# Moving the first two batches' output projection, x1, norm and turn of h2 from the layer stage into the second scan's side work

## The reference, cut to what matters

```
def step(state, xs):                       # the scan, for every batch
    d_t, B_t, C_t, u_t = xs
    dA = jnp.exp(d_t[..., None] * A)
    state = state * dA + (d_t * u_t)[..., None] * B_t[:, None, :]
    y_t = jnp.einsum('ben,bn->be', state, C_t)
...
attn_out = jnp.einsum('hst,thd->shd', att, v).reshape(S, N_HEADS * HEAD_DIM) @ wo
x1 = x + attn_out
h2 = _rms_norm(x1, ln2_w)
mlp = jax.nn.silu(h2 @ w_gate) * (h2 @ w_up) @ w_down
processed = x1 + mlp
gated = gate * processed + (1.0 - gate) * x
```

## Time and profile before

| | us |
|---|---|
| median of 3 runs | 2834.7 (2831.01 to 2835.09) |
| the profiled execution's own time | 2834.77 |
| its span in the profile | 2833.0 |
| PE busy | 2541.2 (90%) |
| PEld busy | 1845.5 (65%) |
| DVE busy | 1963.8 (69%) |
| ACT busy | 1614.7 (57%) |
| POOL busy | 1614.6 (57%) |

### The profile page before, as it was taken

One profiled execution on the slowest core, in us unless ns is written; L12 is line 12 of the kernel. 1 busy time (PEld: TensorE's weight loads), 2 busy tenths in 40 slices (PEclk: granted clock), 3 DMA queues, 4 the chain that ended last, 5 costly groups with the idle time before them and its releaser, 6 DMA issues. The chain is left out here.

```text
span 2833.0 us, 38276 instructions
## 1 busy us (share of the span) xinstructions
PE 2541.2 (90%) x13528; PEld 1845.5 (65%) x13528; DVE 1963.8 (69%) x2505; ACT 1614.7 (57%) x3478; POOL 1614.6 (57%) x898
## 2 busy tenths in 40 slices
...
GB/s 274 254 90 83 74 146 70 123 113 68 141 76 68 153 382 266 285 151 129 105 103 159 105 105 169 93 105 186 93 53 283 286 152 49 89 156 151 154 152 101
DMA packets 249629, 410.43 MB, mean 145 GB/s; under 512 B 50656, under 2 KB 134624, under 8 KB 246624
## 3 DMA queue, kind: packets, MB, share of 16 engines
...
...
## 5 line engine op out<-in xcount | busy, mean ns | idle before, releaser
L696 POOL TENSOR_TENSOR s_x<-s_hp,k_bC 128x1024 f32<-128x1024 f32 x288 | 680.1, 2367 | 48.9 <-DVE s_hp L1152 48.8
L677 POOL TENSOR_TENSOR s_x<-s_du,k_bB 128x1024 f32<-128x1024 f32 x254 | 600.6, 2376 | 13.9 <-DVE s_du L1178 7.6
L803 PE MATMUL s_py<-k_ident,s_x 128*128 128x128 f32 x4096 | 525.1, 274 | 31.1 <-POOL s_x L696 31.0
L803 PEld LDWEIGHTS s_py<-k_ident,s_x 128*128 128x128 f32 x4096 | 462.7, 142 | 46.5 <-POOL s_x L696 42.7
L1076 ACT ACTIVATE s_pA<-s_delta,k_negA 128x512 f32<-128x512 f32 x512 | 333.6, 681 | 172.4 <-DVE s_x L1129 166.9
L1822 PE MATMUL l_p<-l_hT,l_ring 128*128 128x256 f32 x1792 | 389.7, 381 | 1.9 <-ACT l_hT L1928 1.0
L1822 PEld LDWEIGHTS l_p<-l_hT,l_ring 128*128 128x128 f32 x1792 | 342.2, 191 | 49.2 <-issue 1.4
L1076 ACT ACTIVATE s_x<-s_delta,k_negA 128x512 f32<-128x512 f32 x512 | 340.2, 710 | 0.0
L1152 DVE TENSOR_TENSOR_SCAN s_hp<-s_x,s_carry,s_pA 128x512 f32<-128x512 f32 x256 | 321.6, 1267 | 21.8 <-PE s_pA L785 16.1
L977 ACT ACTIVATE s_xT<-s_duT,k_BT 128x128 f32<-128x128 f32 x1024 | 336.4, 389 | 0.1
L1152 DVE TENSOR_TENSOR_SCAN s_hp<-s_x,s_pA 128x512 f32<-128x512 f32 x256 | 309.9, 1211 | 33.8 <-ACT s_x L1076 22.1
...
(10 more groups left out here) (218 smaller groups left out, 3718.9 us busy)
## 6 DMA issues: line engine op xcount, KB each, us to landing
k_bC<-scratch_xd SPq DMA_DIRECT2D x32, 1024.0 KB, 10.4
scratch_ug<-p_ug ACTq DMA_DIRECT2D x16, 1024.0 KB, 4.2
...
```

The source lines that it names most:

```text
L677: pool.tensor_tensor(out=x[:, 4 * g:4 * g + 2], in0=du[:, s % 2:s % 2 + 1].broadcast_to([P, 2, HALF]), in1=bB[:, 2 * g:2 * g + 2], op=ALU. ...
L696: pool.tensor_tensor(out=x[:, 2 * i:2 * i + 2], in0=hp_of(s, i), in1=bC[:, 2 * i:2 * i + 2], op=ALU.mult).then_inc(pool_hc, 1)
L803: last = nc.tensor.matmul(py[:, a], x[:, n, a * P:(a + 1) * P], ident[:], is_transpose=True, start=False, stop=n == NS - 1 and a == HALF / ...
```

## The change: what it does, and the diff

Layer 1 ends with the attention. Its output o stays in `hidden[:, 16:32]`. SP stores the raw base rows and the normed rows `hid` to scratch and loads what scan 2 starts with as soon as the queue gets there, before k, coef and v.

Scan 2 gets 26 slots in a unit instead of 21, in an order of its own: the output projection of the left 512 columns of the result (64 slots, 32 matmuls of 512 columns, from slot 0 in unit 0 to unit 2), a gap of 7 slots, that of the right 512 columns (64 slots, to unit 5), a gap of 40 slots, in which x1, base, mean square, power, norm, and the turn of h2 (16 transposes, units 5 and 6) take place, then gate and up (512 slots, from unit 6 to 26), a gap of 10, and down (128 slots, to unit 31). Before, gate and up ran from unit 0 to 24 and down to unit 30. `wo` comes through the same ring, 16 tiles of 512 KB in the place of 16 tiles of the same size in layer 1. h2T's memory holds the base rows until they are stored. The diagonals of B lie in the tensor of `bB` now; both scans make and use them as before, and the helpers that take `first` give the same numbers for both.

```diff
-FILL = (1, 5, 3, 3, 1, 2, 2, 4)
+FILL = (1, 5, 4, 3, 3, 3, 3, 4)
...
+TILES_WO = H2 * NH // 2
+TILES_UP = TILES_WO + 2 * NI
+TILES_ALL = TILES_UP + NI // 2
+WO_PART = 2 * NH * SPAN
+WO_DONE_0 = fill_slot(WO_PART - 1)
+WO_FROM = (0, fill_from(WO_DONE_0 + 3))
+WO_DONE = (WO_DONE_0, fill_slot(WO_FROM[1] + WO_PART - 1))
+X1_LAG, BASE_LAG = 1, 2
+SQUARE_AT, MEAN_AT, POW_AT, NORM_AT = (WO_DONE[1] + k for k in (4, 4, 5, 8))
+TURN_AT, SPREAD_AT = (WO_DONE[1] + 8, WO_DONE[1] + 10), (WO_DONE[1] + 10, WO_DONE[1] + 12)
 GATE_UP = 2 * NI * KT
-TILES_UP, TILES_ALL = 2 * NI, 2 * NI + NI // 2
+GATE_UP_FROM = fill_from(WO_DONE[1] + 13)
 DOWN_HALF = 2 * NI * SPAN
-DOWN_FROM = GATE_UP + 10
+DOWN_FROM = GATE_UP_FROM + GATE_UP + 10
...
             if fill:
-                sp.dma_start(h2T[:].rearrange("p k r -> p (k r)"), t["h2T0"]).then_inc(h2_in, 16)
-                sp.dma_start(coef[:], t["coef0"]).then_inc(coef_in, 16)
                 for k in range(RING):
                     load_weights(k)
+                sp.dma_start(hid, t["hid0"].rearrange("(a p) c -> p a c", p=P)).then_inc(hid_in, 16)
+                sp.dma_start(base, t["base0"].rearrange("(a p) c -> p a c", p=P)).then_inc(base_in, 16)
...
+                if fill and s == (WO_DONE[1] + BASE_LAG) // NPAIR:
+                    sp.wait_ge(base_ready, H2 * SPAN)
+                    sp.dma_start(t["base0"].rearrange("(a p) c -> p a c", p=P), base).then_inc(base_out, 16)
...
+            def wo(h, k):
+                head, a = k // SPAN, k % SPAN
+                tile = h * NH // 2 + head // 2
+                if k == 0 and h:
+                    pe.wait_ge(x1_ready, SPAN * h)
+                    pe.wait_ge(base_ready, SPAN * h)
+                if k % (2 * SPAN) == 0:
+                    pe.wait_ge(w_in[tile % RING], 16 * (tile // RING) + 16)
+                last = nc.tensor.matmul((p_gate, p_up)[a][:], o[:, head, a * P:(a + 1) * P],
+                                        ring[:, tile % RING, head % 2 * HALF:(head % 2 + 1) * HALF], start=head == 0, stop=head == NH - 1)
+                if k % (2 * SPAN) == 2 * SPAN - 1:
+                    last.then_inc(w_used, 1)
+
+            def turn_h2(j):
+                if j == 0:
+                    pe.wait_ge(x1_ready, SPAN * H2)
+                    pe.wait_ge(base_ready, SPAN * H2)
+                    pe.wait_ge(normed, SPAN)
...
+            def square(b):
+                act.wait_ge(x1_ready, SPAN + b + 1)
+                nc.scalar.activation(normed_rows[:, b], hid[:, b], ACT.Square, accum_out=squares[:, b:b + 1]).then_inc(sq_ready, 1)
...
+            def spread(j, i):
+                act.wait_ge(h2_turned, j + 1)
+                act.wait_ge(ln2_in, 16)
+                act.wait_ge(base_out, 16)
...
     T_DOWN = T_MLP + 2 * NI
-    TILES = T_DOWN + NI if last_half else T_MLP
+    TILES = T_DOWN + NI if last_half else T_WO
...
-                sp.wait_ge(base_ready, 3 * SPAN)
+                sp.wait_ge(base_ready, SPAN)
                 sp.dma_start(t["base0"].rearrange("(a p) c -> p a c", p=P), rows[:]).then_inc(out_done, 16)
-                sp.wait_ge(h2_act, KT // 2)
-                sp.wait_ge(h2_vec, KT // 2)
-                sp.dma_start(t["h2T0"].rearrange("p (k r) -> p k r", r=ROWS), hT[:]).then_inc(out_done, 16)
+                sp.wait_ge(hid_ready, SPAN)
+                sp.dma_start(t["hid0"].rearrange("(a p) c -> p a c", p=P), hid[:]).then_inc(out_done, 16)
...
-            pe.wait_ge(expd, COMBOS)
-            for k in range(NH - APART):
...
-            turn(normed_rows, h2row_ready, turned2)
-
-            if last_half:
+            if last_half:
+                pe.wait_ge(expd, COMBOS)
+                for k in range(NH - APART):
```

More of the change, by code:

```diff
@@ L75, in __init__, with states_by_pool, quad_place @@
         self.ropes = ctx.enter_context(nc.sbuf_tensor(f"c{first}_ropes", [P, SPAN, 2 * DH], F32))
+TURNED, SCALED = (3, 7), {0: (1, 5), SPAN: (1, 5)}
+def states_by_pool(first):
+    return [n for n in range(NS) if n // 2 not in TURNED + SCALED[first]]
+def quad_place(first, g):
+    mine = states_by_pool(first)
+    quad = [n for n in mine if n // 4 == g]
+    return mine.index(quad[0]), len(quad)
 class Kept:
@@ L85, in sb @@
             return ctx.enter_context(nc.sbuf_tensor("k_" + name, shape, F32))
-        self.bB = sb("bB", [P, NS // 2, HALF])
+        self.bB = sb("bB", [P, max(len(states_by_pool(first)) + 2 * len(SCALED[first]) for first in SCALED), HALF])
         self.bC = sb("bC", [P, NS, HALF])
@@ L346 @@
 NPAIR = NS // 2
-FROM_PE = (1, 3, 5, 7)
-TURNED, SCALED = (3, 7), (1, 5)
-FROM_POOL = tuple(i for i in range(NPAIR) if i not in FROM_PE)
-NT, NF, ND_B = 2 * len(TURNED), 2 * len(FROM_PE), 2 * len(SCALED)
+NT = 2 * len(TURNED)
 HP_BUFS = 3
@@ L412, in scan_stage @@
     carry = sb("carry", [P, NE, NS])
+    if scaled:
+        free = len(states_by_pool(first))
+        diagB = bB[:, free:free + ND_B].rearrange("p n (a q) -> p n a q", q=P)
     pA = bank("pA", [P, 4, HALF])
@@ L431, in scan_stage @@
         hidden = keep.hidden
+        o = hidden[:, NH:2 * NH]
+        hid, normed_rows = (hidden[:, KT * k:KT * (k + 1)].rearrange("p m r -> p (m r)").rearrange("p (b d) -> p b d", d=DI) for k in range(2))
+        base = h2T[:].rearrange("p k r -> p (k r)").rearrange("p (b d) -> p b d", d=DI)
+        ln2 = sb("ln2", [P, KT])
+        squares = sb("squares", [P, SPAN])
+        minus_half = sb("minus_half", [P, SPAN])
         ring = sb("ring", [P, RING, KT * P])
@@ L473, in after_vec @@
     def after_vec(s, i):
[L474 removed]
+        return vec_count[s, i]
     def after_carry(s, i):
@@ L690, in times_C @@
             def times_C(s, i):
-                if i not in pool_pairs(s):
+                if i not in pool_pairs(first, s):
                     return
@@ L728, in _ @@
                     begin(s + 1)
-                if last_tile:
-                    make_diagonals(chunk(s) + 1, 1)
+                if last_tile and scaled:
+                    make_diagonals(chunk(s) + 1, scaled[0])
+                if fill:
+                    root(NPAIR * s, NPAIR * s + NPAIR // 2)
                 times_C(s, 3)
@@ L735, in _ @@
                 times_C(s, 5)
-                if last_tile:
-                    make_diagonals(chunk(s) + 1, 5)
+                if last_tile and scaled:
+                    make_diagonals(chunk(s) + 1, scaled[1])
                 quad(s + 1, 1)
@@ L784, in make_b @@
                         else:
-                            last = nc.tensor.matmul(out, duT[:, a * P:(a + 1) * P], diagB[:, 2 * SCALED.index(i) + n % 2, a], start=True, stop=True)
+                            last = nc.tensor.matmul(out, duT[:, a * P:(a + 1) * P], diagB[:, 2 * scaled.index(i) + n % 2, a], start=True, stop=True)
                     last.then_inc(b_ready, 1)
@@ L838, in feed_forward @@
                 for k in range(begin, end):
-                    if k < GATE_UP:
-                        gate_up(k)
+                    for h in range(H2):
+                        if 0 <= k - WO_FROM[h] < WO_PART and (k - WO_FROM[h]) % 2 == 0:
+                            wo(h, (k - WO_FROM[h]) // 2)
+                    if 0 <= k - GATE_UP_FROM < GATE_UP:
+                        gate_up(k - GATE_UP_FROM)
                     at = k - DOWN_FROM
```

297 lines of the change are left out of this document (192 added, 105 removed).

## The result

| | before | changed |
|---|---|---|
| median, us | 2832.86 (2829.88 to 2835.09, 4 runs) | 2810.97 (2808.05 to 2813.41, 4 runs) |
| ratio to before | | 0.9925, interval 0.9910 to 0.9941 |
| the profiled execution's own time | 2834.77 | 2810.57 |
| its span | 2833.0 | 2808.7 |
| first scan of scan 2, to the first scan of unit 31 | 791.2 | 833.4 |

The change makes the kernel 22 us faster by the medians and 24.2 by the two profiled executions. Three sections of the trace account for the difference of the spans: scan 2's first scan starts 67.7 us earlier (1248.02 instead of 1315.74), the 32 units take 42.3 us more (859.44 instead of 817.17, unit 31 taken as 26.0 in both), and what follows them takes 1.1 more (701.2 instead of 700.1).

What follows compares the result with a forecast made beforehand. It took PE to become the bound of nearly every scan 2 unit; -64 us from layer 1 and +46 in scan 2 made -18 on 2834.77, with 1 us for side-chain gaps 2818 us; 8 in 10 range 2798 to 2834.

Steps and rivals of the forecast that it cites:

- What goes from layer 1: End of layer 1: scan 2 starts at 1243.0, 65.3 us earlier; less 1 us for stores, net -64 (-60 to -65).
- a late end of layer 1: Rival: a store, the kept loads or wv's tiles land after the attention; by 10 us it gives 2828; chance 0.05.
- PE becomes the bound: Scan 2's 23 units with 26 slots: PE needs 26.3 us, taken as 26.6 with waits, 612 us in all.
- The light units: Scan 2's units 2, 5, 6 and 26: PE has room, DVE or ACT bounds; 103 us, ends 98 and 108.
- The late tile: Chunk starts: tile issued behind eight column loads, so PE waits 1 to 3 us in unit 8, up to 5 in 16.
- The four first units: Units 0, 8, 16 and 24, which start chunks: 27.2, 30.5, 35 and 29.3, together 122 us, ends 117 and 132.
- The sum: Whole kernel: scan 2's units 863 us against 817.17, +46; with -64 from layer 1, -18 on 2834.77.
- The range: The forecast's own ends: -65 + 37 to -60 + 62, thus 2807 to 2836, mostly 2808 to 2829.
- The signs named ahead: Scan 2 starts near 1243; units 9-15, 17-23 at 26.3 to 27 us; DVE's L1118 wait far above 19.4; unit 5 at most 26.5.
- PE has room: Rival: scan 2 stays bound by DVE and POOL and grows by some 15 us, giving 2786; chance 0.14.
- the rule weighed in the prediction: Skill's rule, not followed: read weight-load share, 80% in scan 2; a fifth of each unit, 5 us, would be free.
- Tiles come late in every unit: Rival: PE waits for ring tiles in each of 27 units of scan 2, 1 us each, giving 2845; chance 0.11.

Runs made afterwards that it cites:

- e2_down_later: The changed kernel with a gap of 17 slots instead of 10 ahead of the down projection, which then begins in unit 27; 2800.4 us.
- e5_narrow: The changed kernel with gate and up matmuls at 128 of their 256 columns, half of that product left out; 2799.0 us.
- e10_all_narrow: The changed kernel with ring tile before load_dt, down 7 slots later, sigmoid and swish one place earlier, and gate/up matmuls at 128 of 256 columns; 2784.9 us.

## Why the prediction was right, step by step

- **What goes from layer 1** (forecast 65.3, net 64; measured 66.9 at the first DMA, 67.7 at the first scan). Of it 1.4 us are from ahead of the attention's end, which comes 1.4 us earlier in this execution, as the layer's first turns do (1067.58 instead of 1068.93). The handover took 1.1 us where 1.3 was taken. The 1 us charged for the two stores and the last tiles was not needed, and the rival of a late end of layer 1 is out.
- **PE becomes the bound** (26.3 us of need, 26.6 a unit). Units 28 to 30 took 26.25 with PE never idle. The 23 full units took 611.9 us in all, forecast 612; but two of them, 9 and 27, took 29.4 and 31.5, and a third, 17, 28.1. The other 20 took 26.1 on the average, so that the charge of 0.3 for small waits was too high and the lumps were missing. The 15.2 us of the scan's own PE work come from units in which POOL was as full as PE (120.52 and 120.56 of 120.91); they held, since 26.25 less 26 x 0.429 is 15.1, in units in which POOL was not full (74.16 of 78.75).
- **The light units** 2, 5, 6 and 26 took 106.0 us, forecast 103. Units 2 and 5 are longer by DVE's four new steps (DVE busy 25.8 and 25.7). Unit 26 is 1.5 us over; the wait ahead of down, of which two thirds lie in it, isn't the reason, since it takes 26.5 too in `e2_down_later`, which has no such wait. POOL is the fullest engine there (25.75 us); the cause is open.
- **The late tile.** The chain was as described, issue behind the column loads, then a wait at the last place of unit 8, 3.09 us where 1 to 3 was forecast. Two details failed. The loss showed in unit 9, since the scans of the next unit had begun, and behind unit 16 no wait for a tile came in this execution, where up to 5 us were charged; five of the variants had one there, of 0.5 to 2.4 us. The four first units took 115.6 us, forecast 122.
- **The down projection's start** is the step that the prediction lacks. It gave units 26 to 30 "0.07 us of it each" from the kernel before and took 26.6 for unit 27. The gap of 10 slots was no longer long enough: at 21 slots a unit it reached from place 2 to place 7, at 26 slots from place 3 to place 6, and POOL's product stands 4 places behind the last up matmul, at place 7, one behind the place where down now begins. PE stood 4.1 us for it. The kernel before had a short wait at the same place, 1.5 us. Cost 5.3 us, 3.3 of them by the clock.
- **The clock** was in no term of the sum. The trace of before had the rows for it: 0.94 and 0.95 in units 8 and 16 of the earlier trace rows.
- **The sum**: 611.9 + 106.0 + 115.6 + 26 = 859.4 for the units, forecast 863, and +42.3 instead of +46. With -67.7 for layer 1 and what stands ahead of it, and +1.1 behind scan 2, that is -24.3 on the span instead of -17. The errors of the terms (+5 in unit 27, +4 in units 9 and 17, -9 in the ordinary units, +3 in the light ones, -6 in the first units) largely cancelled. That the sum for scan 2 came within 4 us is in part luck: it left out two lumps and charged too much for the ordinary units.
- **The range**: the ends of the terms add up to +29 (605 + 98 + 117 + 26.3 - 817.2) and +72, where +37 and +62 were used without a reason given. The measured +42 lies in both.
- **The signs named ahead**: scan 2's first instruction came at 1241.4, 1243 forecast. DVE's wait for PE's sum (L1118, now L882 on PE's side) was to rise far above 19.4 us and stood at 17.9; what rose was its wait for `make_b`, from 10.6 to 31.8. Of the 14 units 9 to 15 and 17 to 23 only four took 26.3 to 27 us, the others lie between 25.0 and 29.4, so the mean was right and the regularity was not. Unit 5 took 26.8, 26.5 at most by the forecast.

**PE has room** was rightly a rival: PE is the bound of the units that were tested, but by no more than 1 us each. I took that with PE out of the way scan 2 would grow by 15 us. From its first scan to unit 31 it grew by 32.0 in `e5_narrow`, with the waits in it, and by 17.7 in `e10_all_narrow`, without them; both keep the full width of the output projection (units 0 to 5) and of down (26 to 31). `e5_narrow` shows 25.4 and 25.8 us a unit with PE relieved of 5.6 us by the count of columns, against 25.2 before, so POOL, DVE and ACT with the gate chains packed closer stand under 1 us behind PE. Seen from there, PE's own need costs the changed kernel 0.7 to 1.0 us a unit, its closer packing 0.2 to 0.6, and the rest of the +42 are the down projection's units, where PE needs 26.25 each, units 0 to 6 (+6.7 us together) and the lumps. That split is read from these two experiments, whose clock was not quite full, so its parts are good to some tenths of a microsecond.

On the rule weighed in the prediction: units 28 to 30 had the weight loads busy 55.57 of 78.75 us, 71%, while PE had no gap and neither DVE (69.32) nor POOL (74.16) was full. The same kind of unit grew from 24.2 us with 21 slots to 26.25 with 26, by 2.07 where five slots of 0.429 are 2.1; that alone would prove less, since at 21 slots POOL was full too. None of the growth vanished into what the weight loads left free. The Trainium skill, "Perfetto Trace Analysis", section "Identifying the Most-Contended Engine", would have had room there; the measurement decides against it for matmuls of 512 columns in float32. In units 10 to 15, whose side work has 256 columns, the weight loads were busy 89% (140.68 of 158.48) beside PE's 99%, and the two measures say nearly the same.

**Tiles come late in every unit** is out: no unit but 9 had such a wait in the changed kernel's trace.
